# Experts of the edge stream on four tiles over two chunks, and the output bias added by VectorE

## The reference, cut to what matters

```
e = leaky_relu(a_src[src] + a_dst[dst], 0.2)
ee = exp(e - segment_max(e, dst)[dst]);  denom = segment_sum(ee, dst)
agg = segment_sum(h[src] * (ee / denom[dst]), dst)        # 16 numbers per token
scores = layernorm(agg + b_gat).reshape(M, 4, 4).mean(1)  # picks 2 of 4 experts
for ei in range(4):
    g  = weight of expert ei for the token, or 0
    hh = gelu(x @ W1[ei] + b1[ei])      # 64 -> 128
    out = out + g * (hh @ W2[ei] + b2[ei])   # 128 -> 64
```

## Time and profile before

| | |
|---|---|
| median of three runs | 3511.93 us |
| the profiled execution | 3511.03 us |
| its span | 3509.2 us |
| busy: TensorE, VectorE | 2667.1 us (76%), 2626.0 us (75%) |
| busy: ScalarE, POOL | 2117.0 us (60%), 2121.5 us (60%) |
| granted TensorE clock, mean | 0.864 |
| edge stream on VectorE | 790 to 2990 us, about 2200 us |

### The profile page before, as it was taken

One profiled execution on the slowest core, in us unless ns is written; L12 is line 12 of the kernel. 1 busy time (PEld: TensorE's weight loads), 2 busy tenths in 40 slices (PEclk: granted clock), 3 DMA queues, 4 the chain that ended last, 5 costly groups with the idle time before them and its releaser, 6 DMA issues. The chain is left out here.

```text
span 3509.2 us, 50874 instructions
## 1 busy us (share of the span) xinstructions
PE 2667.1 (76%) x12450; PEld 2118.4 (60%) x12450; DVE 2626.0 (75%) x7198; ACT 2117.0 (60%) x4084; POOL 2121.5 (60%) x2073
## 2 busy tenths in 40 slices
PE   1666566658888898898888988888988896177773
PEld 1545455446676777677777767777777774044452
DVE  8987888847777776776776766666667777789975
ACT  2666666655565656665666566566656662178884
POOL 7877775036656566666666666766666674745410
PEclk8677777769898999999999999999999998578896
DMA  2111111022222222222221222222222221311102
GB/s 74 23 26 25 25 26 20 2 57 47 54 43 54 50 57 58 54 44 58 54 57 45 58 55 44 58 54 49 52 58 55 49 53 36 103 29 53 28 1 48
DMA packets 172983, 161.27 MB, mean 46 GB/s; under 512 B 73128, under 2 KB 130888, under 8 KB 172104
## 3 DMA queue, kind: packets, MB, share of 16 engines
q1 hardware_dynamic: 108512, 127.47, 11.9%
q0 software_dynamic: 64240, 31.62, 7.8%
HBM read 107.49 MB, written 51.45 MB: 45 GB/s over the span
## 5 line engine op out<-in xcount | busy, mean ns | idle before, releaser
L975 PE MATMUL es_pgot<-parts,es_pick 128*128 128x512 f32 x6528 | 1648.1, 413 | 268.7 <-DVEq L1050 265.4
L877 POOL DMA_INDIRECT es_got<-node_table,late x1360 | 1318.2, 969 | 717.0 <-issue 380.7
L975 PEld LDWEIGHTS es_pgot<-parts,es_pick 128*128 128x128 f32 x6528 | 1294.3, 201 | 558.8 <-issue 284.0
L1048 DVE COPY_PREDICATED es_pgot<-es_bits,es_pgot 128x512 f32<-128x512 int32 (+4 forms) x2040 | 753.3, 369 | 381.8 <-DVE es_got L1049 74.2
L903 ACT ACTIVATE es_pick<-es_away,consts 128x512 fp32r<-128x512 f32 x816 | 521.5, 711 | 284.6 <-PE es_pgot L975 277.2
L299 POOL DMA_INDIRECT fr_ring<-in_emb,fr_rows x384 | 462.6, 1205 | 132.2 <-issue 116.4
L905 ACT ACTIVATE es_pick<-es_pick,consts 128x2048 fp32r<-128x2048 f32 x204 | 409.3, 2007 | 24.2
L1160 DVE TENSOR_TENSOR_SCAN es_st<-es_ex,es_st,es_msg 128x32 f32<-128x32 f32 x1088 | 209.9, 282 | 10.0
L515 DVE TENSOR_TENSOR fr_space<-fr_space 128x1024 f32<-128x1024 f32 x173 | 211.6, 1223 | 5.5 <-DVE fr_space L516 2.4
L516 DVE TENSOR_TENSOR fr_space<-fr_space 128x1024 f32<-128x1024 f32 x173 | 211.1, 1220 | 0.0
L903 ACT ACT_TABLE_LOAD x32 | 41.1, 1283 | 224.0 <-PE es_pgot L975 224.0
(11 more groups left out here) (366 smaller groups left out, 4025.3 us busy)
## 6 DMA issues: line engine op xcount, KB each, us to landing
es_away<-sorted_keys SPq DMA_DIRECT2D x204, 256.0 KB
edge_states<-es_st SPq DMA_DIRECT2D x68, 384.0 KB
es_got<-node_table,late POOLq DMA_INDIRECT x1360
expert_outputs<-ex_y SPq DMA_DIRECT2D x64, 256.0 KB
bk_y<-expert_outputs SPq DMA_DIRECT2D x8, 2048.0 KB, 8.4
fr_ring<-in_emb,fr_rows POOLq DMA_INDIRECT x384, 2.5
out_dram<-h SPq DMA_DIRECT2D x4, 1024.0 KB, 5.1
late<-in_edges SPq DMA_DIRECT2D x1, 2048.0 KB, 9.2
```

What stands on the lines that cost most here:

```text
L877: pool.indirect_dma_start(out=got[:, r, k, :], out_offset=None, in_=table_dram, in_offset=bass.IndirectOffsetOnAxis(ap=src[:, n, k:k + 1]. ...
L975: mm = pe.matmul(p_got[:, (2 * q + c) % BANKS], pick[:, q // 2, k, at * P:at * P + P], parts[:, part, k], start=(k == 0 and part == 0), st ...
L1048: ch.step(v.copy_predicated(at[:, :, 0:half], spread(bits[:, 2 * q:2 * q + 2, b], half), at[:, :, half:2 * half])); pause(dve, s_dve, ch.b ...
```

## The change

Three things are changed together.

1. The experts' unit grows from two tiles with all four experts in a turn to four tiles with two experts in a turn: an even chunk does experts 0 and 1 of four tiles, the odd one experts 2 and 3 of the same tiles. The hidden product is now 256 columns wide instead of 128, with half as many products; one Gelu of 512 columns replaces two of 256. The number of output products stays.
2. The bias products on TensorE are gone. Each output product starts its own sum.
3. ScalarE no longer copies `p_y` to `y`. VectorE does it in one `tensor_tensor` that adds the bias, at the very end of its turn, behind `scores`. It waits for TensorE's second `output` and for the previous store of `y`.

SP's store of `y` keeps its place in SP's order, and writes 512 bytes for each token in place of 1024, for twice as many tokens.

```
-EN = ET * P
+FT = 2 * ET
+EN = FT * P
...
-        hid, y = sb("ex_hid", [P, 2, EN], F32), sb("ex_y", [P, ET, EXPERTS * D], F32)
-        p_hid, p_y = ps("ex_phid", [P, 2, EN]), ps("ex_py", [P, ET, EXPERTS * D])
+        hid, y = sb("ex_hid", [P, ET, EN // ET], F32), sb("ex_y", [P, FT, 2 * D], F32)
+        p_hid, p_y = ps("ex_phid", [P, ET, EN // ET]), ps("ex_py", [P, FT, 2 * D])
...            (ScalarE, in turn)
                     next_pick(0)
                     if with_experts:
-                        pause(act, s_hid_p, c * EXPERTS + 2, s_spent)
-                        for n in range(2):
-                            a.activation(hid[:, n], p_hid[:, n], ACT.Gelu, bias=W("e_b1")[:, n:n + 1]).then_inc(s_hid, 1)
+                        pause(act, s_hid_p, c * 2 + 1, s_spent)
+                        a.activation(hid[:], p_hid[:], ACT.Gelu, bias=W("e_b1")[:, 2 * r:2 * r + 1]).then_inc(s_hid, 1)
...
                     next_pick(2)
-                    if with_experts:
-                        pause(act, s_y_p, c * EXPERTS + EXPERTS, s_spent)
-                        pause(act, s_y_out, c * 16 + 16, s_spent)
-                        a.activation(y[:], p_y[:], ACT.Copy).then_inc(s_y, 1)
...            (TensorE)
-            def expert(c, n):
-                both = xts[:, bass.ds(c, 1)].rearrange("p one n -> p (one n)")
+            def expert(i, n):
+                four = xts[:, bass.ds(i * 2, 2)].rearrange("p two n -> p (two n)")
                 for t in range(ET):
-                    mm = pe.matmul(p_hid[:, n % 2, t * P:t * P + P], W("e_w1_odd" if t else "e_w1")[:, n * HID:n * HID + HID], both, start=True, stop=True)
+                    mm = pe.matmul(p_hid[:, t], W("e_w1_odd" if t else "e_w1")[:, n * HID:n * HID + HID], four, start=True, stop=True)
...            (TensorE, in turn)
                         pause(pe, s_y, c + 1, s_spent)
-                        for t in range(ET):
-                            pe.matmul(p_y[:, t, :], C("ones_row")[0:1], W("e_b2")[0:1], start=(t == 0), stop=False, skip_group_check=True)
-                        output(c, 0)
-                        output(c, 1)
-                        expert(c, 2)
-                        expert(c, 3)
+                        output(c, 2 * r)
+                        expert(i, 2 * r + 1)
...            (VectorE, end of turn)
                         scores(1 - r)
+                    if with_experts:
+                        pause(dve, s_y_p, c * 2 + 2, s_spent)
+                        pause(dve, s_y_out, c * 16 + 16, s_spent)
+                        v.tensor_tensor(y[:], p_y[:], repeat(W("e_b2")[:, 2 * r * D:2 * r * D + 2 * D], FT), ALU.add).then_inc(s_y, 1)
```

More of the change, by code:

```diff
@@ L848, in turn @@
                         pause(sp, s_y, c + 2, s_spent)
-                        sp.dma_start(y_dram.rearrange("(s t p) f -> s p t f", p=P, t=ET)[bass.ds(c, 1)].rearrange("s p t f -> (s p) t f"), y[:]).then_inc(s_y_out, 16)
+                        sp.dma_start(y_dram.rearrange("(s t p) f -> s p t f", p=P, t=FT)[bass.ds(i, 1)].rearrange("s p t f -> (s p) t f")[:, :, r * 2 * D:r * 2 * D + 2 * D], y[:]).then_inc(s_y_out, 16)
             with sp.Fori(0, ESLOTS // 2) as i:
@@ L931, in turn @@
                     if with_experts:
[L932 to L935, removed]
+                        pause(act, s_hid_p, c * 2 + 2, s_spent)
+                        a.activation(hid[:], p_hid[:], ACT.Gelu, bias=W("e_b1")[:, 2 * r + 1:2 * r + 2]).then_inc(s_hid, 1)
                     next_pick(2)
-                    if with_experts:
-                        pause(act, s_y_p, c * EXPERTS + EXPERTS, s_spent)
-                        pause(act, s_y_out, c * 16 + 16, s_spent)
-                        a.activation(y[:], p_y[:], ACT.Copy).then_inc(s_y, 1)
             with act.Fori(0, ESLOTS // 2) as i:
@@ L977, in pair @@
                 mm.then_inc(s_got_p, 1)
-            def expert(c, n):
-                both = xts[:, bass.ds(c, 1)].rearrange("p one n -> p (one n)")
+            def expert(i, n):
+                four = xts[:, bass.ds(i * 2, 2)].rearrange("p two n -> p (two n)")
                 for t in range(ET):
-                    mm = pe.matmul(p_hid[:, n % 2, t * P:t * P + P], W("e_w1_odd" if t else "e_w1")[:, n * HID:n * HID + HID], both, start=True, stop=True)
+                    mm = pe.matmul(p_hid[:, t], W("e_w1_odd" if t else "e_w1")[:, n * HID:n * HID + HID], four, start=True, stop=True)
                 mm.then_inc(s_hid_p, 1)
             def output(c, n):
-                pause(pe, s_hid, c * EXPERTS + n + 1, s_spent)
-                for t in range(ET):
-                    mm = pe.matmul(p_y[:, t, n * D:n * D + D], hid[:, n % 2, t * P:t * P + P], W("e_w2")[:, n * D:n * D + D], start=False, stop=True, skip_group_check=True)
+                pause(pe, s_hid, c * 2 + n % 2 + 1, s_spent)
+                for k in range(FT):
+                    at = k // ET * P
+                    mm = pe.matmul(p_y[:, k, n % 2 * D:n % 2 * D + D], hid[:, k % ET, at:at + P], W("e_w2")[:, n * D:n * D + D], start=True, stop=True)
                 mm.then_inc(s_y_p, 1)
@@ L1003, in turn @@
                     if with_experts:
-                        expert(c, 0)
-                        expert(c, 1)
+                        expert(i, 2 * r)
                     if r < pairs:
@@ L1019, in turn @@
                     if with_experts:
-                        output(c, 2)
-                        output(c, 3)
+                        output(c, 2 * r + 1)
                     if r < pairs:
@@ L1123, in listing, with turn @@
                     dve.sem_inc(s_list, 1)
-            def turn(i, takes=2, listings=None):
+            def turn(i, takes=2, listings=None, with_experts=True):
                 for r in range(2):
@@ L1181, in _ @@
             ch.resume(LOOPED + 1)
-            turn(ESLOTS // 2)
+            turn(ESLOTS // 2, with_experts=False)
             ch.end(LOOPED + 2)
-            turn(TURNS - 1, 1)
+            turn(TURNS - 1, 1, with_experts=False)
             ch.step(v.tensor_copy(mem["last"][:], st[:, 1, CH, :]))
```

## The result

| | before | after |
|---|---|---|
| median | 3511.62 us (4 runs) | 3547.46 us (4 runs, 3546.04 to 3551.12) |
| span of the profiled execution | 3509.2 us | 3544.9 us |
| busy: TensorE, VectorE | 2667.1, 2626.0 us | 2602.3, 2665.3 us |
| first 14 turns on VectorE, written out | 477.9 us | 489.7 us |
| 48 turns of VectorE's loop | 1545.8 us | 1569.7 us |

The ratio is 1.0106, with a 95% interval of 1.0091 to 1.0121. The change was forecast to cost 27 us and costs 36; 3547 us lies just inside the upper end of the forecast's own range. The stretches are taken from the starts of the first VectorE instruction of each turn (L1132, now L1121). Of the 35.7 us between the spans 11.8 us came in the written-out turns and 23.9 us in the loop; outside the stream nothing moved by more than 2 us.

What follows compares the result with a forecast made beforehand. The prediction took VectorE's own instruction list as the bound: 38.9 us for the addition less 10.8 us for shorter branch gaps, 28.1 us on 3511.9, gives 3540, rounded down to 3539 us. Own range 3528 to 3548, 8 in 10 3516 to 3556.

Steps and rivals of the forecast that it cites:

- VectorE's list is the bound, TensorE's savings are idle time: Edge stream: VectorE's instructions, one behind the other, set the turn; bias and hidden products saved on TensorE count 0.
- Addition in the middle of the loop, 0.77 us: 24 turn ends inside VectorE's loop: the new addition and its waits cost 0.77 us each, 18.5 us.
- the 0.6 to 0.8 us that the forecast gave as its sign: Mid-loop and written-out turns: this much more between a turn's reductions and the next one's start would show the forecast right.
- Addition in written-out turns, 0.66 us: 17 turn ends ahead of the loop, behind it and at its last iteration: 0.66 us each, 11.2 us.
- Branch: two waits more, the addition under the fetch, all gaps short: 23 branches of VectorE's loop: waits add 9.2 us, the fetch hides the addition, a later SP load gives 10.8 us back.
- first rival: VectorE's loop branch gets no shorter, or longer, by store of y or shifted code: 3551 us, up to 3559; chance 0.18.
- The second rival, TensorE's slow stretches leaving the sixth pair: More idle time ahead of TensorE's fourth pair ends VectorE's waits for TensorE, 22 us less: 3518 us; chance 0.13.

Runs made afterwards that it cites:

- e1: The changed kernel with four increments of an unused counter ahead of VectorE's loop, which shift the loop's code: 3525.07 us.
- e6: The changed kernel with the addition made twice in the 48 turns of VectorE's loop, the first copy into an idle tile: 3557.85 us.
- e5: The kernel before, with SP's first load of es_away in each turn held until VectorE has written diff: 3502.34 us.
- e2: The changed kernel with SP's store of y moved behind the first load of es_away of the next turn: 3560.53 us.
- f3: The kernel before with VectorE's loop written out and the waits between a take's predicated copies put on the copies themselves: 3275.61 us.
- e7: The kernel before with VectorE's loop of 24 iterations written out as 48 turns: 3383.01 us.

## Why the prediction was right, and where it was off

- *VectorE's list is the bound, TensorE's savings are idle time.* Right. The tiles alone change nothing, 1.0001, and TensorE's waits grew by 99 us.
- *Addition in the middle of the loop, 0.77 us.* The term is right to 0.01 us where no standstill falls on it: in e1 the next turn starts 1.06 us behind the reductions, 0.29 before. In the changed kernel it is 1.40 us, 1.11 more, and so outside the 0.6 to 0.8 us that the forecast gave as its sign.
- *Addition in written-out turns, 0.66 us.* Too low. The first 14 turns grew by 11.8 us, 0.84 each. Two waits ahead of the addition make the gap 0.29 us, where 0.05 on top of the addition was allowed: 0.29 + 0.61 - 0.18 = 0.72. The rest, 0.1 us, wasn't taken apart; one of the 14 additions has a standstill ahead of it (a gap of 0.64 us). Of the same term, the two turns behind the loop were to cost 1.3 us, and the last five turns are 0.8 us shorter instead, unexplained.
- *Branch: two waits more, the addition under the fetch, all gaps short.* Right. From the end of the reductions to the next turn it is 0.44 + 0.69 + 2.63 = 3.76 us in the mean, 3.80 before: 0.04 less, where I had forecast 0.07 less. The experiments show each piece: the hiding (e6) and the load (e5, e2, and the start of the instruction packet). The measured 3547 us lies nearer to the first rival's 3551, in which the branch gets no shorter, than to 3539. By the time alone that rival could not be told from the forecast; the gaps decide against it.
- *Where it was off.* The sum left out what the place of the code costs. The first rival named it ("shift its code unluckily") but tied it to the branch and gave it no price. The change adds 42 sequencer instructions ahead of the loop and ten inside. From the spacing of starts, averaged over the iterations and against e1, the three standstills cost 1.08 us in an iteration after the change and 0.46 before, 0.62 us more; 24 x 0.62 = 15 us. With four instructions added 22 us come back, more than the change had lost there, since these places cost next to nothing.
- *The second rival, TensorE's slow stretches leaving the sixth pair*, happened as a mechanism: 22.4 us of waits became 5.5. What spoke against it, that the idle time ahead of the sixth pair stays as it is, was wrong: pairs four and five end later, and an idle time of over 2.5 us ahead of the sixth came in 25 of the 48 turns of the loop before and in 12 now. It gave only 0.30 us in an iteration, 7 us in the loop. I had priced it at 22, which was too much, because the idle time in such a row includes the hand-over of 0.3 us that is there without any wait: a wait of 0.83 us costs 0.5.

Together for one iteration of the loop: 0.77 + 0.62 - 0.30 - 0.04 = 1.05 us, measured 23.9 / 24 = 1.0. The forecast of +27 us was near the mark in part by luck: a cost and a gain that it lacked, 15 and 7 us, went against each other.

## What to carry to other kernels

Before moving work from one engine to another, ask which of them is waited for, from the waits and not from the busy shares: here 65 us less on TensorE and 49 us less on ScalarE bought nothing, and 40 us more on VectorE cost nearly its whole time. When a short hardware loop sits on the engine that sets the pace, price the loop first: its branch and what else the loop adds to a turn cost 130 us here, more than three times the change. And if two versions differ by less than 1%, shift the loop's code by a few idle instructions before believing either.

## What the runs showed of the hardware

- VectorE's branch back to the head of its loop of 374 to 384 instructions takes 2.8 to 3.2 us until the next instruction, and 3.7 to 4.0 us when SP sent a load of 256 KB 0.4 us ahead of it, because the instruction packet then starts some 1 us later. The loops of the other engines in the kernel before, of 47 instructions (SP), 108 (ScalarE) and 584 (TensorE), go on 0.05 to 0.31 us after theirs.
- VectorE's sequencer stands still for about 0.35 us every 128 instructions, in a loop at the same places in each iteration, and a packet of 8192 bytes on the instruction queue follows. Where a wait or an instruction still running covers the standstill, it costs nothing; elsewhere it is lost. The Trainium skill ("Runtime: NRT & Kernel Launch", Instruction fetch mechanics) speaks of blocks of 256 instructions and calls the crossing mostly hidden; here the spacing is 128 and up to 1.1 us an iteration isn't hidden.
- A wait with its increment, as an instruction of its own between dependent VectorE instructions, costs more than the same wait on the next instruction (f3 against e7): 30 instructions fewer in a turn gave 107 us in 68 turns, about 0.05 us each, with other engines setting part of the pace by then.
